# The norms' reciprocal roots of a two-layer model's first layer, taken on GpSimd by a power; VectorE's statistics in another order

## The reference, cut to what matters

```python
def _layernorm(x, axis=-1, eps=1e-05):
    m = jnp.mean(x, axis=axis, keepdims=True)
    v = jnp.var(x, axis=axis, keepdims=True)
    return (x - m) / jnp.sqrt(v + eps)
...
    x = L0_attn_x                                  # 16 x 256 rows of 128
    xn = _layernorm(x, axis=-1)                    # norm 1: of x
    s = _L0_attn_ref(xn, ...)                      # c = f*c + i*z by step of time,
                                                   # then _layer_norm(c): norm 2, of the carry
    g = _silu(_L0_ffn_ref(xn, ...))                # four trees of 4-way choices, depth 5
    x = x + s * g                                  # the merge
    xn = _layernorm(x, axis=-1)                    # norm 3: of the merged rows, for layer 2
```

## Time and profile before

| | us |
|---|---|
| three runs, median (lowest to highest) | 1480.02 (1478.56 to 1483.22) |
| the profiled execution | 1478.64 |
| its span | 1476.8 |
| PE, DVE, ACT, POOL busy over the span | 1277.1, 1255.6, 1222.5, 915.2 |
| first layer, from the start to the last norm's rows on ScalarE | 0 to about 564 |

### The profile page before, as it was taken

The page is one execution under the profiler, slowest core; times in us unless marked ns, Lnnn a source line. Parts: engine busy times, 40 slices in busy tenths (PEclk is TensorE's granted clock), DMA queues, the critical chain, the costliest instruction groups (busy, mean ns, idle before and its releaser), DMA issues.

```text
span 1476.8 us, 31195 instructions
## 1 busy us (share of the span) xinstructions
PE 1277.1 (86%) x9400; PEld 878.2 (59%) x9400; DVE 1255.6 (85%) x4146; ACT 1222.5 (83%) x3366; POOL 915.2 (62%) x1443
## 2 busy tenths in 40 slices
PE   6998988889897677995799999999999999999986
PEld 3666666666566443442466666666666666666665
DVE  3288898988989983787799999999999999999985
ACT  2368998989989985784698998989989898998985
POOL 0246546464464530577887878778787777878753
PEclk8998999999999687996899999999999999999998
DMA  4269778696787972697010211102111011101243
GB/s 114 101 228 338 249 294 313 224 339 243 272 303 270 390 275 72 181 301 273 22 36 12 46 46 39 42 12 46 46 35 45 14 46 46 35 17 42 71 112 104
DMA packets 152103, 210.18 MB, mean 142 GB/s; under 512 B 68224, under 2 KB 105216, under 8 KB 151808
## 3 DMA queue, kind: packets, MB, share of 16 engines
q0 software_dynamic: 36864, 134.76, 25.0%
q1 hardware_dynamic: 113952, 70.80, 17.4%
q10 hardware_dynamic: 1120, 2.64, 0.5%
HBM read 168.84 MB, written 26.74 MB: 132 GB/s over the span
## 4 chain that ended last, share of the span: by engine, by line
PE 24%; ACT 18%; issue 9%; DVE 1%; POOL 1%; ACTq 0%; DVEq 0%; POOLq 0%
ACT lo_s_ps L1788 6%; PE lo_qk_ps L1483 4%; PE lo_s_ps L1546 4%; PE lo_h_ps L1594 4%; PE lo_o_ps L1584 3%; ACT L1877 3%; ACT lo_sq L1770 2%; PE lo_v_ps L1494 2%; ACT prepared_then_rounds L1848 2%; PE lo_s_ps L1533 1%; PE lo_h_ps L1606 1%; ACT prepared_then_rounds L1796 1%; PE lo_o_ps L1516 1%; PE lo_ft_ps L1566 1%; PE lo_o_ps L1566 1%
## 5 line engine op out<-in xcount | busy, mean ns | idle before, releaser
L341 POOL DMA_INDIRECT wide<-in_table,l_idx x128 | 128.6, 1005 | 194.5 <-DVE l_idx L818 130.5
L1788 ACT ACTIVATE lo_s_ps<-lo_s_ps,lo_nmx,lo_rn 128x128 f32<-128x128 f32 x504 | 219.4, 440 | 2.0 <-DVE lo_nmx L2102 1.6
L341 POOL DMA_INDIRECT l_rows<-in_table,l_idx x128 | 129.8, 1014 | 75.4 <-DVE l_idx L825 38.8
L659 ACT ACTIVATE l_rows<-l_rows,l_act 128x128 f32<-128x128 f32 x512 | 153.1, 387 | 1.0
L659 ACT ACTIVATE wide<-wide,l_act 128x128 f32<-128x128 f32 x512 | 153.1, 387 | 1.0
L776 DVE CUSTOM_DVE_ANT_0 wide<-wide,xn_tok 128x128 f32<-128x128 f32 x512 | 142.6, 346 | 5.3 <-DMA wide<-in_table,l_idx 5.3
L440 PE MATMUL l_S<-pre,l_AT 128*128 128x144 f32 (+3 forms) x832 | 127.5, 304 | 20.2 <-ACT l_AT L650 20.2
L440 PEld LDWEIGHTS l_S<-pre,l_AT 128*128 128x128 f32 (+2 forms) x832 | 114.8, 204 | 49.7 <-ACT l_AT L650 36.1
L776 DVE CUSTOM_DVE_ANT_0 l_rows<-l_rows,xn_tok 128x128 f32<-128x128 f32 x512 | 142.7, 346 | 1.1 <-DMA l_rows<-in_table,l_idx 1.1
L1977 POOL TENSOR_TENSOR lo_de_kS<-lo_de_S,lo_de_ops 128x384 f32<-128x384 f32 x128 | 135.3, 1057 | 10.0
L416 PE MATMUL l_log<-l_xT,top_in 128*128 128x512 f32 (+1 forms) x192 | 112.5, 678 | 18.9 <-ACT l_AT L650 18.1
(11 more groups left out here) (328 smaller groups left out, 3661.5 us busy)
## 6 DMA issues: line engine op xcount, KB each, us to landing
lo_VE<-lo_V SPq DMA_DIRECT2D x64, 128.0 KB, 2.4
scratch_ops<-prepared_then_rounds SPq DMA_DIRECT2D x4, 1792.0 KB, 7.0
lo_de_ops<-scratch_ops SPq DMA_DIRECT2D x16, 448.0 KB, 4.1
lo_de_qo<-scratch_qo SPq DMA_DIRECT2D x16, 256.0 KB, 4.5
scratch_qo<-prepared_then_rounds SPq DMA_DIRECT2D x7, 512.0 KB, 8.4
x_tok<-in_x SPq DMA_DIRECT2D x8, 256.0 KB, 5.5
wide<-in_table,l_idx POOLq DMA_INDIRECT x128, 6.0
l_rows<-in_table,l_idx POOLq DMA_INDIRECT x128, 6.2
```

The costliest lines, as they stand in the source:

```text
L341: pool.indirect_dma_start(rows[L][:, r % SLOTS, p, :], None, a[f"table{L}"], bass.IndirectOffsetOnAxis(ap=at[:, p:p + 1], axis=0)).then_in ...
L659: ins = act.activation(z, z, ACT.Copy, scale=actv[L][:, r % 2, k:k + 1])
L1788: ins = act.activation(here, here, ACT.Exp, scale=rn[:, v % 2, j, 2 * k + e:2 * k + e + 1], bias=nmx[:, j, e, k:k + 1], accum_out=sums[:, ...
```

## The change

`rsqrt` and its 12 instructions go from VectorE, and so does the product with the mean. VectorE ends `norms` with the aggregation, which releases the new semaphore `moments`. GpSimd's new function `roots(r)` waits for it and issues four small instructions: minus the mean, variance plus epsilon, that to the power of -0.5, and the product, which releases `scaling`. `roots(g + 2)` is the last thing in GpSimd's iteration g, and the loop starts at -2 instead of 0. In `norms`, the statistics of x and of the carry now stand ahead of the wait for `f_turned` and the merge. The product has a buffer of its own, so that it no longer overwrites the halved variances.

```diff
-def rsqrt(dve, ch, out, v, half_eps, half, bits, a):
-    ch.link(dve.scalar_tensor_tensor(half, v, 0.5, half_eps, ALU.mult, ALU.add))
-    ...
-    for _ in range(3):
-        ch.link(dve.tensor_tensor(a, out, out, ALU.mult))
-        ch.link(dve.tensor_tensor(a, a, half, ALU.mult))
-        ch.link(dve.scalar_tensor_tensor(out, a, 1.5, out, ALU.subtract, ALU.mult))
...
+            def roots(r):
+                if r not in norm_rounds:
+                    return
+                cols = norm_cols(r)
+                v = slice(cols[0], cols[-1] + 1)
+                pool.wait_ge(moments.sem, moments.after(norm_rounds.index(r)))
+                ch.mark(pool.tensor_scalar(nmean[:, v], mv[:, v, 0], -1.0, None, ALU.mult))
+                ch.link(pool.tensor_tensor(veps[:, v], mv[:, v, 1], eps_row[:, v], ALU.add))
+                if r:
+                    pool.wait_ge(scaled_rows.sem, scaled_rows.after(norm_rounds.index(r) - 1))
+                ch.link(pool.tensor_tensor(rstd[:, v], veps[:, v], power[:, v], ALU.pow))
+                pool.tensor_tensor(nmr[:, v], nmean[:, v], rstd[:, v], ALU.mult).then_inc(scaling.sem, 1)
+
-            for g in range(NG + 2):
+            for g in range(-2, NG + 2):
...
                 if on(g - 1):
                     gather(5, GT * (g - 1) + 2)
+                roots(g + 2)
...
             def norms(r):
...
+                if hx is not None:
+                    dve.wait_ge(x_in[hx].sem, 16)
+                    for j in range(GT):
+                        n = ch.mark(dve.bn_stats(stats[:, j, :], m["x_tok"][:, hx * GT + j, :]))
+                if hc is not None:
+                    dve.wait_ge(c_turned.sem, c_turned.after(hc))
+                    for j in range(GT):
+                        n = ch.mark(dve.bn_stats(stats[:, GT + j, :], tp[:, j * P:(j + 1) * P]))
                 if hm is not None:
                     x = m["x_tok"][:, hm * GT:(hm + 1) * GT, :]
                     dve.wait_ge(f_turned.sem, f_turned.after(hm))
                     dve.scalar_tensor_tensor(x, acc[hm % 2][:], 0.25, x, ALU.mult, ALU.add).then_inc(merged.sem, 1)
...
-                rsqrt(dve, ch, rstd[:, v], mv[:, v, 1], half_eps[:, v], half[:, v], bits[:, v], aa[:, v])
-                dve.scalar_tensor_tensor(nmr[:, v], mv[:, v, 0], -1.0, rstd[:, v], ALU.mult, ALU.mult).then_inc(scaling.sem, 1)
+                    ins = dve.bn_aggr(mv[:, k, :], stats[:, k, :])
+                ins.then_inc(moments.sem, 1)
```

More of the change, by code:

```diff
@@ L167, in flat @@
     return ap.rearrange("p a b -> p (a b)")
-RSQRT_OPS = 12
-def rsqrt(dve, ch, out, v, half_eps, half, bits, a):
-    ch.link(dve.scalar_tensor_tensor(half, v, 0.5, half_eps, ALU.mult, ALU.add))
-    ch.link(dve.tensor_scalar(bits, half.bitcast(I32), 1, None, ALU.logical_shift_right))
-    ch.link(dve.tensor_scalar(out.bitcast(I32), bits, -1.0, float(0x5F3759DF - 2 ** 31 - 2 ** 22), ALU.mult, ALU.add))
-    for _ in range(3):
-        ch.link(dve.tensor_tensor(a, out, out, ALU.mult))
-        ch.link(dve.tensor_tensor(a, a, half, ALU.mult))
-        ch.link(dve.scalar_tensor_tensor(out, a, 1.5, out, ALU.subtract, ALU.mult))
 def layer0_phase(nc, m, scr, a):
@@ L210, in layer0_phase @@
         n_, th, t_ = (sb("l0_" + k, [P, GT, D]) for k in ("n", "th", "t"))
-        half_eps = sb("l0_half_eps", [P, 3 * GT])
+        eps_row, power = sb("l0_eps_row", [P, 3 * GT]), sb("l0_power", [P, 3 * GT])
         w["pen"] = th[:, 0, :]
         stats, mv = sb("l0_stats", [P, 3 * GT, 6]), sb("l0_mv", [P, 3 * GT, 2])
-        half, aa, rstd = (sb("l0_" + k, [P, 3 * GT]) for k in ("half", "aa", "rstd"))
-        nmr, bits = half, aa[:].bitcast(I32)
+        veps, nmean, rstd, nmr = (sb("l0_" + k, [P, 3 * GT]) for k in ("veps", "nmean", "rstd", "nmr"))
         tp = ps("l0_tp", [P, 512])
@@ L249, in layer0_phase @@
         pre_early, pre_in, weights_in = ctx.semaphore("pre_early_in"), ctx.semaphore("pre_in"), ctx.semaphore("weights_in")
-        scaling, scaled_rows = st("norm_scaling"), st("norm_rows")
+        moments, scaling, scaled_rows = st("norm_moments"), st("norm_scaling"), st("norm_rows")
         multiplied = st("bias_multiplied")
+        norm_cols = lambda r: [k * GT + j for k, h in enumerate((r, r - 3, r - 4)) if 0 <= h < NG for j in range(GT)]
         norm_rounds = [r for r in range(NG + 4) if 0 <= r < NG or 0 <= r - 4 < NG]
@@ L323, in _ @@
         def _(pool):
+            ch = Chain(ctx, nc, pool, "l0_pool", 0)
             for k, eps in enumerate((EPS, 4 * EPS, EPS)):
-                pool.memset(half_eps[:, k * GT:(k + 1) * GT], 0.5 * eps).then_inc(eps_set, 1)
+                pool.memset(eps_row[:, k * GT:(k + 1) * GT], eps).then_inc(eps_set, 1)
+            pool.memset(power[:], -0.5).then_inc(eps_set, 1)
+            pool.wait_ge(eps_set, 4)
             pool.wait_ge(early, 16 * len(EARLY0))
@@ L853, in norms @@
                 hx, hc, hm = (h if on(h) else None for h in (r, r - 3, r - 4))
+                cols = norm_cols(r)
+                if not cols:
+                    return
+                if hx is not None:
[6 more added lines that the diff above has]
+                        n = ch.mark(dve.bn_stats(stats[:, GT + j, :], tp[:, j * P:(j + 1) * P]))
                 if hm is not None:
@@ L857, in norms @@
                     dve.scalar_tensor_tensor(x, acc[hm % 2][:], 0.25, x, ALU.mult, ALU.add).then_inc(merged.sem, 1)
[L858 to L869, removed]
                     dve.wait_ge(merged.sem, merged.after(hm))
@@ L872, in norms @@
                         n = ch.mark(dve.bn_stats(stats[:, 2 * GT + j, :], m["x_tok"][:, hm * GT + j, :]))
-                    cols += range(2 * GT, 3 * GT)
-                if not cols:
-                    return
                 if r:
-                    dve.wait_ge(scaled_rows.sem, scaled_rows.after(norm_rounds.index(r) - 1))
+                    dve.wait_ge(scaling.sem, scaling.after(norm_rounds.index(r) - 1))
                 ch.wait(n)
                 for k in cols:
[L880 to L884, removed]
-                rsqrt(dve, ch, rstd[:, v], mv[:, v, 1], half_eps[:, v], half[:, v], bits[:, v], aa[:, v])
-                dve.scalar_tensor_tensor(nmr[:, v], mv[:, v, 0], -1.0, rstd[:, v], ALU.mult, ALU.mult).then_inc(scaling.sem, 1)
+                    ins = dve.bn_aggr(mv[:, k, :], stats[:, k, :])
+                ins.then_inc(moments.sem, 1)
             for g in range(NG + 4):
```

## The result

The changed kernel takes 1506.33 us (median of 4 runs, 1504.74 to 1508.97) against 1480.38 (4 runs, 1478.56 to 1483.22) for the kernel before beside it: ratio 1.0179, 95% interval 1.0165 to 1.0192. It is slower by 26 us, 1.8%, where the forecast had 13.6. The profiled execution took 1507.0 with a span of 1505.2, which is 28.4 more than before's span.

What follows compares the result with a forecast made beforehand. ScalarE's queue was taken to set the beat in rounds 4 to 8. Fill +1.2, rounds 4 to 7 +11.7, round 8 +3.3 and drain -2.6 made +13.6 us on 1478.6: 1492, range 1480 to 1506.

Steps and rivals of the forecast that it cites:

- Where the beat is: Steady rounds 4 to 8: ScalarE's queue sets the beat, and a longer wait at `put_rows` moves everything.
- Where the roots come to stand: GpSimd's queue: roots start 0.30 us behind the eighth transfer, end 1.76 us behind it; `put_rows` 4.1 to 6.7 us later.
- Rival A: VectorE's earlier finish reaches GpSimd, so gathers and roots come earlier: about -10 us, 1468; chance 0.12.
- VectorE's lead: After the merge VectorE goes on 4.4 us earlier than before; this is spent in waits for TensorE.
- The power: GpSimd's root chain: taken as 0.5 us, between bounds of 0.24 and 1.535 us.
- the fill: First rounds: +1.2 us in round 0, where nothing overlaps; 0 taken for rounds 1 to 3.
- Rival C: A software power of several us on GpSimd: 1498 at 1.535 us, 1507 at 3 us; chance 0.18 beyond 1499.
- Round 3: Rows ready some 4.9 us later, but ScalarE then idled 3.84 us for a gate and more behind it: 0.
- What is given back: ScalarE's vanished pick wait returns 1.2 us in each of rounds 4 to 7; 2.7 returned in round 8.
- Drain: Last rounds: -1.5 us for an earlier last gather and -1.1 in round 11, together -2.6.
- Rival B: ScalarE's other idle time absorbs the delay: +4 us, 1483; chance 0.15.
- The load of about 6 us: Round 0: if GpSimd's power needed a first-call code load, nothing would cover it, and the time would be 1498.

Runs made afterwards that it cites:

- both edits: The changed kernel with a multiplication in place of the power and roots(g + 2) ahead of the last gather: 1467.76 us, ratio 0.9914.
- the second experiment: The changed kernel with roots(g + 2) one place earlier in GpSimd's iteration, ahead of the level 5 gather: 1481.74 us, ratio 1.0017.

## Why the prediction was right or wrong

**Where the beat is: right.** ScalarE's wait at `put_rows` decides. A steady round is 57 to 59 us of ScalarE's other time plus its wait for the roots at the end, in the mean of rounds 4 to 7: before 58.7 + 2.1, the changed kernel 57.1 + 9.3, with the multiplication 57.8 + 7.2, with both edits 57.4 + 0.8.

**Where the roots come to stand: right.** They start 0.04 us behind the eighth transfer (forecast 0.30), long after the aggregation. Moving one gather behind them took back 24.6 us. Rival A needed the roots to start when the aggregation ends, and fell: GpSimd's wait for TensorE in the iteration ahead of `roots(5)` is 2.54 us, as the 2.49 of the earlier trace rows; and VectorE's lead ended in its waits for TensorE, 6.99 us ahead of `choose(·, 0)` in round 5, where the row of before in round 6 had 1.25. Timeline of the changed kernel, GpSimd and VectorE:

```profile
247.66 0.94 POOL L329 DMA_INDIRECT wide<-in_table,l_idx  x1 [2.54 <-PE l_acc L476]
...
296.71 0.23 DVE L785 TENSOR_REDUCE l_mx<-l_tp 128x16 f32<-128x64 f32 x1 [6.99 <-PE l_tp L442]
```

**The power: the term that was mis-sized most.** The step "I take 0.5, near the lower, since the operand has at most 12 columns" failed, and so did its upper bound, the longest TENSOR_TENSOR in the trace with 1.535 us. Measured by number of columns, timeline of GpSimd, rounds 0, 3 and 5 (the last is shown above):

```profile
9.63 1.04 POOL L342 TENSOR_TENSOR l_rstd<-l_veps,l_power 128x4 f32<-128x4 f32 x1
...
125.36 1.68 POOL L342 TENSOR_TENSOR l_rstd<-l_veps,l_power 128x8 f32<-128x8 f32 x1
```

The bound came from another operation of the same name, and an operation's name doesn't bound its price. The other three instructions were near the forecast (0.39, 0.25 and 0.28). From the transfer's end to the end of the chain go 3.4 us, not 1.76: 1.63 more in each of rounds 4 to 7, and 1.0 more in round 8 with its eight columns (2.75 in all), together 7.5. Exchanging the power for a multiplication was worth 11.3, which has the fill and rounds 2 and 3 in it. Rival C, dear power, holds in this part: it gave 1498 at 1.535 us and 1507 at 3 us, and at 2.31 us it lies between. But it is only part of the miss, and 1506.3 near its 1507 is partly chance: the terms below have their share.

**Round 3: 0 was wrong.** ScalarE's 3.84 us wait for the gate did go, and yet the last transfer of round 4's iteration ends at 189.99 where it ended at 185.44, 4.55 later. The fill's +1.2 is in that, as forecast; the other 3.35 is round 3's. Its start of `put_rows` slipped by 7.0 us (127.58 against 120.58), where the forecast had some 4.9 and counted on the idle time behind it to take up all of it. Why 3.35 us of it got through is not shown by a run.

**What is given back: subtracted from the wrong chain.** I let ScalarE's vanished wait for picks shorten each round by 1.2. It did vanish, nearly: from 120 to 480 us ScalarE waited 2.0 us for picks where it had been 8.1. But the changed kernel's round is GpSimd's: from ScalarE's start through TensorE, VectorE and the gathers to GpSimd's last transfer, and then the roots. From the start of `put_rows` to the end of that transfer go 62.5, 64.8, 63.1 and 64.0 us in rounds 4 to 7 before (mean 63.6), 64.0, 62.2, 64.1 and 62.2 in the changed kernel (63.1), and 63.7 with the multiplication. It gave back 0.5 or nothing. With the 3.4 us behind it, this makes 66.5, and rounds 4 to 7 are 66.4 in the mean (193.41 to 458.90). What ScalarE saves elsewhere in the round, it waits for roots longer. Against 63.6 - 1.2 = 62.4 that is 0.7 a round, 2.8 over the four.

**Drain: nearly right.** From round 8's start to the end 4.2 us are given back (32.6 to 28.4), where the forecast had 2.7 + 2.6 = 5.3.

Together: 3.35 + 7.5 + 2.8 + 1.1 = 14.75 us above the forecast. The spans differ by 28.4 where 13.6 was forecast, 14.8 more. Rival B, the absorbed delay, fell: ScalarE's idle time elsewhere did shrink, and it bought nothing.

**The load of about 6 us** that the Trainium skill ("GPSIMD Engine Reference", section 2.1 Instruction dispatch) puts on the first call into freshly loaded code doesn't show here: the first power starts at 9.63, 0.07 us behind the instruction ahead of it, and takes 1.04 us, as the later one with four columns does.

**The clock: 1.6 to 1.9 us in some rounds, but not what made the changed kernel slower.** In the changed kernel rounds 4 and 6 take 67.4 and 67.5 us at a granted clock of 0.87, rounds 5 and 7 take 65.6 and 65.0 at 0.93. Most of the difference arises in TensorE's products ahead of `choose(·, 0)`. Timeline of TensorE in rounds 4 and 5, then windows of both, each 30 us behind ScalarE's start (columns as above, the granted clock third from the end):

```profile
225.16 1.90 PE L442 MATMUL l_S<-pre,l_AT 128*128 128x144 f32 x8
226.99 1.97 PE L418 MATMUL l_log<-l_xT,top_in 128*64 128x512 f32 x2
...
292.25 1.25 PE L442 MATMUL l_S<-pre,l_AT 128*128 128x144 f32 x8
293.43 1.07 PE L418 MATMUL l_log<-l_xT,top_in 128*64 128x512 f32 x2
```

```profile
223.41:228.41 5.00, 4.20 (x12) 1.96 (x12) 0.00 (x0) 4.97 (x14) 0.00 (x0) 0.72 0.00 0
290.81:295.81 5.00, 4.50 (x22) 2.58 (x22) 0.00 (x0) 4.97 (x14) 0.00 (x0) 1.00 0.00 0
```

The same products take some 1.5 us more in round 4, and VectorE waits for them. The choice starts 37.8 us behind ScalarE's start in round 4 and 35.9 in round 5, the gather that waits for its group's indices 41.1 and 39.2. So there the low clock lies on the path that sets the round. At the start of a round it is low as well (0.50 from 265 to 270 us, the lower of its two levels, 1.2 GHz, right behind a stall of 6.84 us), but costs this path nothing that shows: in the second experiment's kernel round 7 runs at 1.00 throughout, and its choice starts 35.9 us behind ScalarE's start too.

The kernel before has the low stretch at 30 us in three of these four rounds (granted clock 0.77, 0.66 and 0.73 in rounds 5, 6 and 7), the changed kernel in two. Of the loops given above, those with the stretch are 64.0 us in the mean before and 64.0 in the changed kernel, those without it 62.5 and 62.2. So the stretch explains none of the loss against before, and rounds at like clock gave back 0.3 us or nothing of the 1.2. The multiplication's kernel has it in all four rounds (0.66), which takes some of the gain that its trace could show. This is read from traces: no run changed the clock alone. What brings the stretch about isn't shown; TensorE's stalls ahead of it are alike in rounds 4 and 5 (6.88 and 6.84 us, then 2.12 in both).

**Where VectorE's lead went.** It ends at that choice, in waits of 6.99 to 8.77 us for TensorE, where it waited 1.2 us or not at all before. With the low stretch in both kernels, the gather behind comes 0.9 us earlier than before (41.1 against 42.0 us behind ScalarE's start). From there to the eighth transfer's end go 22.9 to 23.0 us, where it was 21.1 to 22.8; GpSimd's wait for TensorE's sums in that stretch is 1.92 or 2.54 us, where it was 0.84 to 2.49. That is how far the traces show it; no run of its own tested it.

## What to carry to other kernels

Before work goes to an engine with idle time, look at what stands ahead of it in that engine's queue at the moment it is due: the busy share of 63% said that there was room, and the place in the queue was worth 24.6 us. Measure an unknown operation before it is put on the path, and don't bound it by others that share its instruction's name. And when a wait becomes the longest in the round, work out the length of the new loop that it closes; idle time given back on the engine that waits there is not time gained. Compare rounds at like granted clock: two rounds of one kernel differed by 1.8 us here, more than some of the terms that were sought.

## What the runs showed of the hardware

GpSimd's power on 128 partitions takes 1.04, 1.68 and 2.31 us for 4, 8 and 12 columns: some 0.16 us a column and 0.4 ahead of them. A multiplication in its place, on twelve columns, takes 0.21. Behind ScalarE's start in round 5 of the changed kernel the timeline of TensorE shows:

```profile
263.98 1.09 PE L378 MATMUL l_tp<-ident,xn_tok 128*128 128x128 f32 x4 [6.84 <-ACT l_n L668]
266.94 2.08 PE L418 MATMUL l_log<-l_xT,top_in 128*128 128x512 f32 x2 [1.02 <-ACT l_AT L652]
```

And the window around them (columns as above, the granted clock third from the end):

```profile
265.00:270.00 5.00, 3.98 (x18) 2.50 (x17) 5.00 (x31) 4.72 (x14) 3.97 (x4) 0.50 0.95 318
```

The four turned blocks take 1.09 us where they took 0.63 before (0.95 us of idle ahead of them in round 6), and a pair of 512-column products 2.08 where it took 1.12. In the multiplication's run this came after stalls of 4.67 to 4.71 us too (1.08 and 1.09 us for the four), and after one of 4.66 us it did not (0.63), so the length of the stall alone does not tell.
